# A first router whose bias goes through the matrix unit, whose gates ScalarE scales, and whose rows are stored and loaded in two batches

## The chip, the cores and the metric

One core of a Trainium2 chip runs the program. The metric is the device time of one execution in microseconds (us); lower is better. The engines are named as the profile names them: PE is the matrix unit (PEld its weight loads), DVE is VectorE, ACT is ScalarE, POOL is GpSimd, and SP issues the transfers.

## What is computed

Two transformer layers on x of 2 x 1024 tokens of width 128, all in float32 with a residual sum after each of four parts. Of the parts the change touches the second, a mixture of 160 experts of which each token takes 8:

```
logits = x @ router_w.T + expert_bias
probs  = sigmoid(logits)
top_w, top_idx = top_k(probs, 8)
top_w  = top_w / (sum(top_w) + 1e-9) * 2.5
combine[token, top_idx] = top_w
h1  = silu(einsum('th,eih->eti', x, w_gate)) * combine.T[:, :, None]
out = einsum('eti,ehi->th', h1, w_down) + silu(x @ w_gate_shared.T) @ w_down_shared.T
```

Here x is the layer norm of the residual. The first part is attention with 16 heads of width 8, the third a memory that is updated in 16 steps, the fourth a mixture of 8 experts with a router of its own.

## The kernel before

The four parts run one after the other. The 2048 tokens are 16 tiles of 128 rows, worked on in G = 4 groups of 4 tiles (512 tokens). The order of the work is written out by hand per engine: each engine has its own program, the programs meet at counting semaphores, and within an engine everything runs in the order written.

**Norm.** `norm(1)` makes the layer norm before the first mixture. DVE computes statistics and `xn` group by group (L1440 to L1452), PE transposes each group into bank 0 or 1 (L1027), and ACT copies the bank twice, to `xh` (rounded to the fast matmul type, L810) and to `xnT` (L811). DVE then makes the low parts `xl = xnT - xh` of all four groups (`low_x`, L1467). In the expert loop every product is three products: xh by both weight parts, xl by the high one.

**First router.** PE makes the logits of a group, four products of 160 columns (`router_logits`, L1224), in two banks of a pair of `wide`; group g + 2 reuses the banks of group g. DVE adds the bias into `gates` (L1654), ACT takes the sigmoid in place (L931). Only after all four bias sums does DVE choose: per group four MAX8 (L1660), four MATCH_REPLACE that strike out the eight largest (L1667), sum, epsilon, reciprocal and factor (L1668 to L1671), then `left = max(left, 0) - gates` (L1673), which leaves minus the chosen gates, and a multiply by the factor of the token (L1675). Meanwhile PE and ACT do the shared expert in banks 4 and 5 (L1234, silu L939, L1214). When a group is chosen PE transposes its 4 x 160 columns (L1247, L1248), and ACT copies them out as `cT_first` (128 experts) and `cT_last` (32 experts, L943, L944).

**Rows through DRAM.** SP stores each group's columns to `c_dram` (L586, L588). Once all eight stores have landed it loads rows back, spread over the partitions: one load of 1 MB per pair of experts (`load_rows`, L571) into one of CB = 4 buffers `cb`.

**Expert loop.** 80 pairs of experts by 4 groups are 320 steps. In a step PE makes three products into one of four banks (L1259), ACT the silu (L958), DVE multiplies by the row (L1693), ACT rounds to `hh` (L952), DVE makes `hl` (L1685), and PE accumulates a low product (L1266) and two high ones (L1272) of earlier steps. PE's low product in iteration n waits until DVE has ended step n - 2. PE begins the loop when `cT_ready` is complete and all `xl` are there.

The second router (layer 2) uses the same `norm` and `low_x` in `norm(3)`.

## Time and profile before

| what | value |
|---|---|
| median of 3 runs | 1117.31 us (1117.04 to 1119.65) |
| profiled execution, its own time | 1117.76 us |
| its span (first to last instruction) | 1115.8 us |
| PE, DVE, ACT, POOL busy | 93%, 75%, 72%, 20% of the span |
| attention ends, first router's stage, expert loop starts | about 340, 350 to 391, 391 |
| second router's stage | about 934 to 968 |
| PE's share of the chain that ended last | 82% |

Busy shares are averages over stages. In the two expert loops and in attention PE is nearly always busy. The stage that the change rewrites is some 40 us long, and there the chain of waits runs over DVE and the transfers. [...]

### The profile page before, as it was taken

Reading aid. Unit: us, or ns where it says so; the run is one execution under the profiler, and the core shown is the slowest. Engines: PE = TensorE matmul, PEld = TensorE weight load, DVE = VectorE, ACT = ScalarE, POOL = GpSimd, SP = SyncE. Lnnn points to the kernel's source line nnn. Section 1 sums busy time; section 2 is a strip of 40 time slices with the busy share of each in tenths; the row PEclk is TensorE's granted clock in tenths of the full one; section 3 lists DMA queues with packets and bytes.
Section 4 is the critical chain, followed back from the end, with each engine's and each line's share of the span. In section 5 each row is a group of like instructions: output and inputs, shape, how many; then the busy total and the mean of one; then the engine's idle time right before and its main releaser. Section 6 shows DMA issues by size and latency. Waiting matters only on the chain.

```text
span 1115.8 us, 20193 instructions
## 1 busy us (share of the span) xinstructions
PE 1039.4 (93%) x5244; PEld 688.9 (62%) x5244; DVE 831.3 (75%) x1965; ACT 804.8 (72%) x1310; POOL 222.3 (20%) x326
## 2 busy tenths in 40 slices
PE   5899999999996589999999999999998998799997
PEld 3222222232325278888888888888876777587785
DVE  8544444343345779999999999999986887598897
ACT  6599999999992468787878787877774443266664
POOL 3767664444442000000000000000004112000000
PEclk9799999999997899999999999999999998799999
DMA  4368776666661176666666666666621000123321
GB/s 142 116 213 259 221 235 204 208 208 216 210 211 42 36 301 238 235 244 244 240 249 239 239 237 235 240 248 245 239 79 41 1 1 1 59 99 117 111 86 38
DMA packets 91894, 190.43 MB, mean 171 GB/s; under 512 B 10700, under 2 KB 55372, under 8 KB 81612
## 3 DMA queue, kind: packets, MB, share of 16 engines
q1 hardware_dynamic: 91860, 190.05, 49.9%
q8 instruction: 12, 0.20, 0.1%
q14 instruction: 22, 0.18, 0.1%
HBM read 154.03 MB, written 35.98 MB: 170 GB/s over the span
## 4 chain that ended last, share of the span: by engine, by line
PE 82%; DVE 8%; ACT 4%; issue 3%; DMA 2%; POOL 2%; ACTq 0%; DVEq 0%; SPq 0%; POOLq 0%
PE bank L1259 26%; PE bank L1272 15%; PE bank L1129 10%; PE bank L1266 8%; PE bank L1111 6%; PE bank L1114 6%; ACT ring L897 2%; PE bank L1361 2%; PE bank L1140 1%; POOL m_norm L786 1%; PE bank L1345 1%; DVE xn L1452 1%; DMA ring<-c_rows 1%; DVE stats L1440 1%; PE bank L1077 1%
## 5 line engine op out<-in xcount | busy, mean ns | idle before, releaser
L897 ACT ACTIVATE ring<-bank,minus_bound 128x1024 f32<-128x1024 f32 x256 | 271.4, 1111 | 22.9 <-DVE bank L1553 11.9
L1259 PE MATMUL bank<-xh,w_parts 128*128 128x512 f32 x896 | 277.2, 391 | 1.9 <-DVEq L1679 1.9
L958 ACT ACTIVATE bank<-bank 128x512 f32<-128x512 f32 x320 | 186.2, 582 | 90.8 <-PE bank L1259 90.8
L1693 DVE TENSOR_TENSOR bank<-bank,ring 128x512 f32<-128x512 f32 x320 | 223.9, 700 | 29.7 <-DMA ring<-c_rows 6.8
L1272 PE MATMUL bank<-hh,w_parts 128*128 128x512 f32 x776 | 239.7, 390 | 0.0
L1685 DVE TENSOR_TENSOR hl<-bank,hh 128x512 fp32r<-128x512 f32 x321 | 218.6, 681 | 0.1
L1553 DVE TENSOR_TENSOR bank<-bank,corner 128x128 f32<-128x128 f32 x256 | 76.6, 299 | 170.4 <-PE bank L1114 170.2
L952 ACT ACTIVATE hh<-bank 128x512 fp32r<-128x512 f32 x321 | 190.4, 593 | 3.2 <-DVE bank L1693 3.1
L1259 PEld LDWEIGHTS bank<-xh,w_parts 128*128 128x128 f32 x896 | 167.9, 188 | 38.0 <-DVEq L1679 2.3
L1259 PE MATMUL bank<-xl,w_parts 128*128 128x512 f32 x448 | 174.7, 390 | 0.0
L1272 PEld LDWEIGHTS bank<-hh,w_parts 128*128 128x128 f32 x776 | 145.9, 188 | 30.6 <-ACT hh L952 0.4
L1266 PE MATMUL bank<-hl,w_parts 128*128 128x512 f32 x390 | 153.5, 394 | 6.5 <-DVE hl L1685 6.4
L1129 PE MATMUL bank<-ring,v_cur 128*32 128x512 f32 x1024 | 137.2, 608 | 0.7 <-ACT ring L897 0.7
L1114 PE MATMUL bank<-q_stack,k_stack 128*128 128x512 bf16 (+3 forms) x384 | 106.7, 333 | 1.5 <-ACTq L890 1.5
L1111 PE MATMUL bank<-q_stack,k_stack 128*128 128x384 bf16 (+2 forms) x320 | 98.3, 323 | 7.4 <-ACT ring L897 3.4
L1259 PEld LDWEIGHTS bank<-xl,w_parts 128*128 128x128 f32 x448 | 84.4, 188 | 17.7
L766 POOL MEMSET ring<- 128x512 f32 x1 | 0.5, 531 | 473.1 <-PE bank L1266 473.1
L1111 PEld LDWEIGHTS bank<-q_stack,k_stack 128*128 128x128 bf16 x320 | 30.7, 97 | 97.6 <-ACT ring L897 92.1
L1266 PEld LDWEIGHTS bank<-hl,w_parts 128*128 128x128 f32 x390 | 73.4, 188 | 26.9 <-DVE hl L1685 12.0
L1114 PEld LDWEIGHTS bank<-q_stack,k_stack 128*128 128x128 bf16 x384 | 34.0, 99 | 58.2 <-ACT ring L897 28.5
L1008 ACT ACTIVATE q_stack<-bank 128x512 f32<-128x512 f32 x64 | 38.2, 597 | 27.3 <-PE bank L1259 25.5
L952 ACT ACTIVATE hh<-q_stack 128x512 fp32r<-128x512 f32 x65 | 41.0, 630 | 16.6 <-DVE q_stack L1849 15.5
(281 smaller groups left out, 1135.4 us busy)
## 6 DMA issues: line engine op xcount, KB each, us to landing
ring<-c_rows SPq DMA_DIRECT2D x80, 1024.0 KB, 5.0
w_parts<-w_pairs SPq DMA_DIRECT2D x160, 128.0 KB, 2.5
w_pairs<-xh SPq DMA_DIRECT2D x16, 768.0 KB, 4.4
q_stack<-q_parts SPq DMA_DIRECT2D x64, 144.0 KB
k_stack<-k_parts SPq DMA_DIRECT2D x192, 48.0 KB
w_pairs<-xl SPq DMA_DIRECT2D x16, 512.0 KB, 2.9
ring<-c_rows SPq DMA_DIRECT2D x16, 512.0 KB, 4.6
big<-in_w_exp SPq DMA_DIRECT2D x16, 384.0 KB, 4.8
```

The lines of the kernel that those rows point to most:

```text
L897: act.activation(ring[:, c % RING * S:(c % RING + 1) * S], wide[c % 2][:], ACT.Exp, bias=minus_bound[:]).then_inc(exp_done, 1)
L952: act.activation(hh[(c - 1) % 2][:], hidden, ACT.Copy).then_inc(split, 1)
L958: act.activation(bank(4 + c % ZB), bank(4 + c % ZB), ACT.Silu).then_inc(silu_ready, 1)
L1111: ins = pe.matmul(wide[c % 2][:, lo:mid], k_stack[0][u][:, keys], q_stack[1][u][:, lo:mid], start=True, stop=True)
L1114: ins = pe.matmul(wide[c % 2][:, mid:hi], k_stack[1][u][:, keys], q_stack[0][u][:, mid:hi], start=True, stop=True)
L1129: ins = pe.matmul(bank(4 + u)[at:at + 32, :], v_cur[u][:, done_step % QT, :], ring[:, at_ring + h * 512:at_ring + (h + 1) * 512], start=(d ...
L1259: ins = pe.matmul(out_, w[i], x_[j], start=start and k == 0, stop=stop and k == 2, skip_group_check=not start)
L1266: return pe.matmul(bank(done_step % G), w[0], hl[done_step % 2][:], start=False, stop=False, skip_group_check=True)
L1272: ins = pe.matmul(bank(done_step % G), part, hh[done_step % 2][:], start=False, stop=False, skip_group_check=True)
L1553: dve.tensor_tensor(tile, tile, corner[:], ALU.mult).then_inc(corner_done, 1)
L1685: dve.tensor_tensor(hl[(c - 1) % 2][:], hidden, hh[(c - 1) % 2][:].bitcast(F32), ALU.subtract).then_inc(split, 1)
L1693: dve.tensor_tensor(bank(4 + c % ZB), bank(4 + c % ZB), cb[u][:, g * GW:(g + 1) * GW], ALU.mult).then_inc(hid_ready, 1)
```

## The change

- **Bias.** PE opens each group's logit banks with two products of a row of ones by the bias (320 columns each, `router_biases`), and the logits accumulate on top. Those of groups 0 and 1 stand ahead of `norm(1)`; those of groups 2 and 3 wait for the sigmoid of groups 0 and 1. ACT takes the sigmoid directly from the banks (`take_logits`), between its copies of xnT. The DVE sums are gone. The sigmoid table is loaded early by a one-column activation.
- **High and low parts of x.** ACT makes `xh` from `xnT` after the last sigmoid (`high_x`); DVE makes the low parts after the choice. The same holds for the second router, where `high_x` follows one group behind.
- **Choice.** Epsilon and factor are one instruction and the multiply by the factor is gone from DVE: ACT scales each tile (`Copy` with a scale per token, 16 instructions of 160 columns). `rest` has four buffers instead of two.
- **Shared expert.** All four silus come before the scaling, in banks 2 and 3, and the four down products follow in one piece, ahead of the transposes.
- **Copies.** ACT alternates scaling and copying; `cT_last` of the last group is copied by DVE.
- **Rows.** SP stores groups 0 and 1, waits for them to land, loads their half of the rows for all four buffers (4 x 512 KB), stores groups 2 and 3, waits, and loads the other half. DVE waits for a half at the first and third step of each pair. In the loop each row load is two of 512 KB.
- Several semaphores of the unused slow attention path share those of the fast path.

SP's transfers between the router and the loop, before:

```order
L586 DMA c_rows<-xn 128x512 [waits cT_ready]
L588 DMA c_rows<-fold 32x512 [waits cT_ready]
L586 DMA c_rows<-xn 128x512 [waits cT_ready]
L588 DMA c_rows<-fold 32x512 [waits cT_ready]
L586 DMA c_rows<-xn 128x512 [waits cT_ready]
L588 DMA c_rows<-fold 32x512 [waits cT_ready]
L586 DMA c_rows<-xn 128x512 [waits cT_ready]
L588 DMA c_rows<-fold 32x512 [waits cT_ready]
L571 DMA ring<-c_rows 128x1x2048 [waits c_saved]
L571 DMA ring<-c_rows 128x1x2048 x3
```

and with the change:

```order
L593 DMA c_rows<-xn 128x512 [waits cT_ready]
L594 DMA c_rows<-fold 32x512
L593 DMA c_rows<-xn 128x512 [waits cT_ready]
L594 DMA c_rows<-fold 32x512
L575 DMA ring<-c_rows 128x1x1024 [waits c_saved]
L575 DMA ring<-c_rows 128x1x1024 x3
L593 DMA c_rows<-xn 128x512 [waits cT_ready]
L594 DMA c_rows<-fold 32x512
L593 DMA c_rows<-xn 128x512 [waits cT_end,cT_ready]
L594 DMA c_rows<-fold 32x512
L575 DMA ring<-c_rows 128x1x1024 [waits c_saved]
L575 DMA ring<-c_rows 128x1x1024 x3
```

Four row loads and a wait for `c_saved` now stand ahead of the stores of groups 2 and 3.

ACT from the end of attention to the loop, with the change (xn in L957 is `cT_first`, fold in L959 is `cT_last`):

```order
L823 ACTIVATE xh<-xnT 128x512 [waits xnT_ready] x3
L951 ACT_TABLE_LOAD [waits shared_psum]
L951 ACTIVATE q_stack<-bank 64x512 [waits moe_zero]
L951 ACTIVATE q_stack<-bank 64x512 [waits shared_psum]
L951 ACTIVATE k_stack<-bank 64x512 [waits shared_psum] x2
L964 ACTIVATE ring<-ring,top_inv 128x160 [waits combine_ready]
L964 ACTIVATE ring<-ring,top_inv 128x160 x3
L964 ACTIVATE ring<-ring,top_inv 128x160 [waits combine_ready]
L964 ACTIVATE ring<-ring,top_inv 128x160 x3
L957 ACTIVATE xn<-bank 128x512 [waits cT_psum]
L959 ACTIVATE fold<-bank 32x512
L964 ACTIVATE ring<-ring,top_inv 128x160 [waits combine_ready]
```

The copies of a group stand behind the silus and behind the scaling of the next group; before, only the silus stood ahead of them.

The diff, cut to its core:

```diff
@@ -172,9 +172,10 @@
-        rest = [ring[:, (5 + u) * S:(5 + u) * S + TPG * NE].rearrange("p (t e) -> p t e", t=TPG) for u in range(2)]
+        rest = [ring[:, (2 * g + 1) * S:(2 * g + 1) * S + TPG * NE].rearrange("p (t e) -> p t e", t=TPG) for g in range(G)]
         top = sb("top", [P, NT, 8])
         top_sum = sb("top_sum", [P, NT])
+        early_table = sb("early_table", [P, 1])
         top_inv = sb("top_inv", [P, NT])
@@ -204,6 +205,7 @@
         act_out = [q_stack[0][u][:].bitcast(F32) for u in range(2)]
+        shared_hid = act_out + [k_stack[0][u][:].bitcast(F32) for u in range(2)]
         hid = [q_stack[1][u][:].bitcast(F32) for u in range(2)]
...
...
@@ -566,9 +570,10 @@
-            def load_rows(m, u):
-                sp.dma_start(cb[u], bass.AP(c_dram.tensor, m * (2 * T), [[0, EI], [T, 2], [1, T]])).then_inc(cb_loaded[u], 16)
+            def load_rows(m, u, h):
+                sp.dma_start(cb[u][:, h * S:(h + 1) * S], bass.AP(c_dram.tensor, m * (2 * T) + h * S, [[0, EI], [T, 2], [1, S]]))\
+                    .then_inc((cb_early, cb_loaded)[h][u], 16)
@@ -582,18 +587,21 @@
                 cols = slice(g * GW, (g + 1) * GW)
-                sp.wait_ge(cT_ready, 2 * g + 1)
+                sp.wait_ge(cT_ready, min(2 * g + 2, 2 * G - 1))
+                if g == G - 1:
+                    sp.wait_ge(cT_end, 1)
                 sp.dma_start(c_dram[0:P, cols], cT_first[:, cols]).then_inc(c_saved, 16)
-                sp.wait_ge(cT_ready, 2 * g + 2)
                 sp.dma_start(c_dram[P:NE, cols], cT_last[:, cols]).then_inc(c_saved, 16)
-            sp.wait_ge(c_saved, 2 * G * 16)
-            for u in range(CB):
-                load_rows(u, u)
+                if g % 2:
+                    sp.wait_ge(c_saved, 2 * (g + 1) * 16)
+                    for u in range(CB):
+                        load_rows(u, u, g // 2)
                     sp.wait_ge(hid_ready, i * (CB * G) + ((u + 1) * G + CREDIT))
-                    load_rows(i * CB + (CB + u), u)
+                    for h in range(2):
+                        load_rows(i * CB + (CB + u), u, h)
                     sp.wait_ge(low_used, i * (CB * G) + ((u + 1) * G + 3 + CREDIT))
@@ -799,20 +807,20 @@
-            def norm(k):
+            def norm(k, follow):
                 for g in range(G):
                     cols = slice(g * GW, (g + 1) * GW)
-                    if k == 1 and g == 0:
-                        act.wait_ge(w_saved[0], 16 + NH // 2 * 16)
-                    if k % 2:
-                        act.activation(xh[:, cols], bank(n % 2), ACT.Copy)
                     act.activation(xnT[:, cols], bank(n % 2), ACT.Copy).then_inc(xnT_ready, 1)
-                    if k == 2 and g:
-                        token_gates(g - 1)
-                if k == 2:
-                    token_gates(G - 1)
+                    if g:
+                        follow(g - 1)
+            def high_x(g, k=3):
+                cols = slice(g * GW, (g + 1) * GW)
+                act.wait_ge(xnT_ready, G * k + g + 1)
+                act.activation(xh[:, cols], xnT[:, cols], ACT.Copy).then_inc(xh_ready, 1)
@@ -924,24 +932,40 @@
-            norm(1)
-            for g in range(G):
-                ts = slice(g * TPG, (g + 1) * TPG)
-                act.wait_ge(logit_ready, g + 1)
-                act.activation(gates[:, ts, :], gates[:, ts, :], ACT.Sigmoid).then_inc(gate_ready, 1)
+            act.activation(early_table[:], half[:, 0:1], ACT.Sigmoid)
+            def take_logits(g):
+                act.wait_ge(logit_psum, g + 1)
+                act.activation(gates[:, g * TPG:(g + 1) * TPG, :].rearrange("p (b t) e -> p b t e", b=2),
+                               logits1(g).rearrange("p b (t e) -> p b t e", t=2), ACT.Sigmoid).then_inc(gate_ready, 1)
+            norm(1, take_logits)
+            take_logits(G - 1)
+            act.wait_ge(w_saved[0], 16 + NH // 2 * 16)
+            for g in range(G):
+                high_x(g, 1)
+            act.wait_ge(moe_zero, 1)
             for g in range(G):
                 act.wait_ge(shared_psum, g + 1)
-                if g >= 2:
-                    act.wait_ge(shared_down, g - 1)
-                if g < 2:
-                    act.wait_ge(moe_zero, 1)
-                act.activation(act_out[g % 2][0:EI], bank(4 + g % 2)[0:EI, :], ACT.Silu).then_inc(shared_act, 1)
-            for g in range(G):
+                act.activation(shared_hid[g][0:EI], bank(2 + g % 2)[0:EI, :], ACT.Silu).then_inc(shared_act, 1)
+            def take_cT(g):
                 act.activation(cT_first[:, cols], bank(4 + g % 2), ACT.Copy).then_inc(cT_ready, 1)
-                act.activation(cT_last[:, cols], bank(6 + g % 2)[0:NE - P, :], ACT.Copy).then_inc(cT_ready, 1)
+                if g < G - 1:
+                    act.activation(cT_last[:, cols], bank(6 + g % 2)[0:NE - P, :], ACT.Copy).then_inc(cT_ready, 1)
+            for g in range(G):
+                act.wait_ge(combine_ready, g + 1)
+                for t in range(TPG):
+                    act.activation(rest[g][:, t, :], rest[g][:, t, :], ACT.Copy, scale=top_inv[:, g * TPG + t:g * TPG + t + 1])\
+                        .then_inc(scaled_ready, 1)
+                if g:
+                    take_cT(g - 1)
+            take_cT(G - 1)
             act.sem_inc(silu_ready, CREDIT)
...
@@ -993,9 +1018,10 @@
-            norm(3)
+            norm(3, high_x)
             act.wait_ge(shifted, 1)
             act.activation(soft[:], soft[:], ACT.Exp).then_inc(exp2_ready, 1)
+            high_x(G - 1)
             act.wait_ge(c2T_psum, 1)
@@ -1209,46 +1235,51 @@
-            def shared_sum(g):
-                pe.wait_ge(shared_act, g + 1)
-                pe.matmul(bank(g), wd_shared[:], act_out[g % 2][0:EI], start=True, stop=False, skip_group_check=True)\
-                    .then_inc(shared_down, 1)
+            def router_biases(g):
+                row_ = b_router[0:1, :]
+                for b in range(2):
+                    pe.matmul(logits1(g)[:, b, :], ones[0:1, :], bass.AP(row_.tensor, row_.offset, [list(row_.ap[0]), [0, 2], [1, NE]]),
+                              start=True, stop=False, skip_group_check=True)
                 pe.wait_ge(xnT_ready, G + g + 1)
-                if g >= 2:
-                    pe.wait_ge(logit_ready, g - 1)
                 for t in range(TPG):
                     ins = pe.matmul(logits1(g)[:, t // 2, t % 2 * NE:(t % 2 + 1) * NE], xnT[:, (g * TPG + t) * P:(g * TPG + t + 1) * P],
-                                    w_router[:], start=True, stop=True)
+                                    w_router[:], start=False, stop=True, skip_group_check=True)
                 ins.then_inc(logit_psum, 1)
+                if g < G - 2:
+                    pe.wait_ge(gate_ready, g + 1)
+                    router_biases(g + 2)
+            for g in range(2):
+                router_biases(g)
             norm(1, router_logits)
             for g in range(G):
+                if g == 0:
+                    pe.wait_ge(x_ready, G)
                 if g >= 2:
                     pe.wait_ge(shared_act, g - 1)
+                pe.matmul(bank(2 + g % 2)[0:EI, :], w_shared[:], xnT[:, g * GW:(g + 1) * GW], start=True, stop=True)\
+                    .then_inc(shared_psum, 1)
+            pe.wait_ge(shared_act, G)
+            for g in range(G):
+                pe.matmul(bank(g), wd_shared[:], shared_hid[g][0:EI], start=True, stop=False, skip_group_check=True)
+            for g in range(G):
                 if g == 0:
-                    pe.wait_ge(logit_ready, G)
-                pe.matmul(bank(4 + g % 2)[0:EI, :], w_shared[:], xnT[:, g * GW:(g + 1) * GW], start=True, stop=True)\
-                    .then_inc(shared_psum, 1)
-                if g:
-                    shared_sum(g - 1)
-            shared_sum(G - 1)
-            for g in range(G):
-                pe.wait_ge(combine_ready, g + 1)
-                if g == 0:
-                    pe.wait_ge(shared_act, G)
-                    pe.wait_ge(logit_ready, G)
+                    pe.wait_ge(gate_ready, G)
                 if g >= 2:
                 for t in range(TPG):
-                    pe.transpose(bank(4 + g % 2)[:, t * P:(t + 1) * P], rest[g % 2][:, t, 0:P], ident[:])
-                    ins = pe.transpose(bank(6 + g % 2)[0:NE - P, t * P:(t + 1) * P], rest[g % 2][:, t, P:NE], ident[:])
+                    pe.wait_ge(scaled_ready, g * TPG + t + 1)
+                    pe.transpose(bank(4 + g % 2)[:, t * P:(t + 1) * P], rest[g][:, t, 0:P], ident[:])
+                    ins = pe.transpose(bank(6 + g % 2)[0:NE - P, t * P:(t + 1) * P], rest[g][:, t, P:NE], ident[:])
                 ins.then_inc(cT_psum, 1)
             pe.wait_ge(moe_zero, 1)
-            pe.wait_ge(cT_ready, 2 * G)
+            pe.wait_ge(cT_ready, 2 * G - 1)
+            pe.wait_ge(cT_end, 1)
             pe.wait_ge(xl_ready, G)
@@ -1454,14 +1485,10 @@
                         ins.then_inc(xn_ready, 1)
-                if k % 2:
-                    for g in range(G):
-                        low_x(k, g)
                 cols = slice(g * GW, (g + 1) * GW)
-                dve.wait_ge(xnT_ready, G * k + g + 1)
+                dve.wait_ge(xh_ready, k // 2 * G + g + 1)
                 if k == 1 and g == 0:
@@ -1645,13 +1672,6 @@
             norm(1)
-            dve.wait_ge(w1_loaded, 4 * 16)
-            bias4 = bass.AP(b_router[:].tensor, b_router[:].offset, [list(b_router[:].ap[0]), [0, 2], [0, 2], [1, NE]])
-            for g in range(G):
-                dve.wait_ge(logit_psum, g + 1)
-                v = gates[:, g * TPG:(g + 1) * TPG, :].rearrange("p (b t) e -> p b t e", b=2)
-                dve.tensor_tensor(v, logits1(g).rearrange("p b (t e) -> p b t e", t=2), bias4, ALU.add).then_inc(logit_ready, 1)
             for g in range(G):
@@ -1659,22 +1679,21 @@
                 link.wait()
-                if g >= 2:
-                    dve.wait_ge(cT_psum, g - 1)
-                left = rest[g % 2]
+                left = rest[g]
                 for t in tiles:
                 link(dve.tensor_reduce(top_sum[:, ts], top[:, ts, :], AX.X, ALU.add))
-                link(dve.tensor_scalar(top_sum[:, ts], top_sum[:, ts], 1e-9, None, ALU.add))
-                link(dve.reciprocal(top_inv[:, ts], top_sum[:, ts]))
-                link(dve.tensor_scalar(top_inv[:, ts], top_inv[:, ts], -ROUTED, None, ALU.mult))
-                link(dve.scalar_tensor_tensor(left[:, :, :], left[:, :, :], 0.0, gates[:, ts, :], ALU.max, ALU.subtract))
-                inv = top_inv[:, ts]
-                dve.tensor_tensor(left[:, :, :], left[:, :, :],
-                                  bass.AP(inv.tensor, inv.offset, [list(inv.ap[0]), list(inv.ap[1]), [0, NE]]), ALU.mult).then_inc(combine_ready, 1)
-            dve.wait_ge(cT_ready, 2 * G)
+                link(dve.tensor_scalar(top_sum[:, ts], top_sum[:, ts], 1e-9, -1.0 / ROUTED, ALU.add, ALU.mult))
+                link.sign(dve.reciprocal(top_inv[:, ts], top_sum[:, ts]))
+                link.wait()
+                dve.scalar_tensor_tensor(left[:, :, :], left[:, :, :], 0.0, gates[:, ts, :], ALU.max, ALU.subtract).then_inc(combine_ready, 1)
+            for g in range(G):
+                low_x(1, g)
+            dve.wait_ge(cT_psum, G)
+            dve.tensor_copy(cT_last[:, (G - 1) * GW:G * GW], bank(6 + (G - 1) % 2)[0:NE - P, :]).then_inc(cT_end, 1)
+            dve.wait_ge(cT_end, 1)
+            dve.wait_ge(cT_ready, 2 * G - 1)
             dve.memset(bank(4 + ZB - 1), 0.0).then_inc(hid_ready, CREDIT)
@@ -1687,8 +1706,8 @@
                     n, u, g = i * (CB * G) + c, c // G, c % G
-                    if g == 0:
-                        dve.wait_ge(cb_loaded[u], i * 16 + 16)
+                    if g % 2 == 0:
+                        dve.wait_ge((cb_early, cb_loaded)[g // 2][u], i * 16 + 16)
                     ready(dve, silu_ready, n)
@@ -1829,6 +1848,8 @@
             dve.tensor_tensor(combine2[:], combine2[:], by_row(r_sum[:], NE2), ALU.mult).then_inc(combine2_ready, 1)
+            for g in range(G):
+                low_x(3, g)
             dve.wait_ge(c2T_psum, 1)
```

## Rows read from the trace of the kernel before

**Rows 1.** Chain that ended last, stretch 365 to 440: start us, us, what.
```profile
390.19 2.17 DMA c_rows<-fold
...
392.37 5.23 DMA ring<-c_rows
```
**Rows 2.** Timeline, DVE, 360 to 374: start, us, engine line op.
```profile
361.12 1.89 DVE L1467 TENSOR_TENSOR xl<-xnT,xh 128x512 fp32r<-128x512 f32 x3
...
364.18 1.55 DVE L1654 TENSOR_TENSOR big<-bank,b_router 128x640 f32<-128x640 f32 x2
...
368.34 0.99 DVE L1660 MAX8 top<-big 128x8 f32<-128x160 f32 x4
...
372.24 0.83 DVE L1675 TENSOR_TENSOR ring<-ring,top_inv 128x640 f32<-128x640 f32 x1
```
**Rows 3.** Timeline, PE and ACT, 357 to 378 (x8: four products).
```profile
357.88 2.34 PE L1224 MATMUL bank<-w_router,xnT 128*128 128x160 f32 x8
...
360.73 1.25 PE L1224 MATMUL bank<-w_router,xnT 128*128 128x160 f32 x8
...
361.82 0.60 PE L1027 MATMUL bank<-ident,xn 128*128 128x128 f32 x4
...
365.03 1.47 ACT L931 ACTIVATE big<-big 128x640 f32<-128x640 f32 x2 [0.19 <-DVE big L1654]
...
369.21 1.28 ACT L939 ACT_TABLE_LOAD   x1
...
372.20 1.07 PE L1234 MATMUL bank<-xnT,w_shared 128*64 128x512 f32 x2
...
373.31 0.59 ACT L939 ACTIVATE q_stack<-bank 64x512 f32<-64x512 f32 x1 [1.73 <-PE bank L1234]
...
375.25 1.98 PE L1214 MATMUL bank<-q_stack,wd_shared 64*128 64x512 f32 x4
```
**Rows 4.** Timeline, ACT: two copies of a bank, and two scaled copies at 867.
```profile
389.10 0.60 ACT L943 ACTIVATE xn<-bank 128x512 f32<-128x512 f32 x1 [4.47 <-PE bank L1248]
389.59 0.57 ACT L944 ACTIVATE fold<-bank 32x512 f32<-32x512 f32 x1
...
867.25 0.90 ACT L993 ACTIVATE ring<-state,steps 128x256 f32<-128x256 f32 x2
```
**Rows 5.** Timeline, SP, 388 to 396: the four row loads before the loop.
```profile
392.37 2.49 SPq L571 DMA_DIRECT2D ring<-c_rows  x4
```
**Rows 6.** DMA issues at 392.4, at 393.7 to 394.5, and at 970.2: KB each, median us to landing.
```profile
ring<-c_rows SPq DMA_DIRECT2D x1, 1024.0 KB, 5.2
...
ring<-c_rows SPq DMA_DIRECT2D x2, 1024.0 KB, 10.6
...
ring<-c_rows SPq DMA_DIRECT2D x1, 512.0 KB, 4.2
```
**Rows 7.** Timeline: PE's third low product, third multiply of the expert loop, PE's fifth low product.
```profile
399.06 0.50 PE L1266 MATMUL bank<-hl,w_parts 128*128 128x512 f32 x1 [2.70 <-DVE hl L1685]
...
400.12 0.69 DVE L1693 TENSOR_TENSOR bank<-bank,ring 128x512 f32<-128x512 f32 x1
...
401.92 0.39 PE L1266 MATMUL bank<-hl,w_parts 128*128 128x512 f32 x1
```
**Rows 8.** Stretches: us, PE, PEld, DVE, ACT, POOL busy, PE's clock, DMA share, GB/s.
```profile
350.00:352.50 2.50, 0.03 (x1) 0.00 (x0) 2.40 (x12) 0.00 (x0) 0.37 (x2) 1.00 0.00 0
352.50:355.00 2.50, 0.21 (x1) 0.24 (x2) 2.15 (x13) 0.00 (x0) 2.19 (x3) 0.75 0.00 0
...
393.00:395.00 2.00, 2.00 (x7) 1.58 (x6) 0.00 (x0) 0.70 (x2) 0.00 (x0) 0.57 0.67 172
...
397.00:399.00 2.00, 0.00 (x0) 0.00 (x0) 1.28 (x3) 0.55 (x2) 0.00 (x0) 1.00 1.06 446
```
**Rows 9.** Part 5 of the page, the row multiply of the expert loop.
```profile
L1693 DVE TENSOR_TENSOR bank<-bank,ring 128x512 f32<-128x512 f32 x320 | 223.9, 700 | 29.7 <-DMA ring<-c_rows 6.8
```
**Rows 10.** Timeline, DVE, around the second router.
```profile
950.40 0.29 DVE L1801 TENSOR_REDUCE r_max<-bank 128x16 f32<-128x128 f32 x1 [1.40 <-PE bank L1378]
...
966.50 1.21 DVE L1833 COPY fold<-bank 8x1024 f32<-8x1024 f32 x1 [3.67 <-PE bank L1386]
```

23 lines of the change are left out of this document (13 added, 10 removed).

## The prediction

> **What bounds the kernel now.** I read the page first: PE is busy 93% of the span and has 82% of the chain, so only a stage in which PE waits can be shortened. The chain of the stretch 365 to 440 shows one: from the end of the norm to the expert loop the chain runs over DVE's choice and then over two transfers, the last store of the rows (2.17 us) and the first load (5.23 us) [rows 1]. The timeline shows what DVE does there. It is free of the norm at 361.1, makes four low parts at 0.63 apiece, then four bias sums of some 0.8, and begins to choose only at 368.3; a group takes from 368.34 to 373.07, 4.7 us [rows 2], and the fourth ends at 387.05. The columns are out at 390.2, the rows are there at 397.6 [rows 1], DVE makes its third multiply of the loop at 400.12 and PE its fifth low product at 401.92 [rows 7]. From then on PE goes at its own pace, some 1.4 a step (two from 399.06 to 401.92 [rows 7]), so what PE's fifth low product gains or loses is what the program gains or loses. I follow the change to that instruction.
>
> **Gates.** ACT now has only one copy of a group ahead of the sigmoid, but PE and ACT take turns: bias products of group g + 2 wait for the sigmoid of group g, and the transposes of the next groups are queued behind them. PE's first four products are unchanged and end at 360.2 (357.88 + 2.34, at the low clock) [rows 3]. Two bias products have 640 columns in float32, as four logit products have, so 1.25 [rows 3]. The sum from 360.2: sigmoid 0.74, bias 1.25, transposes 0.60, logits 1.25, sigmoid 0.74, bias 1.25, transposes 0.60, logits of groups 2 and 3 2.50, sigmoid 0.74 [rows 3], and some 0.2 of handovers: the last gates are ready at 370.1, those of group 2 at 368.9.
>
> **Choice.** DVE begins at 361.2 instead of 368.3, since low parts and bias sums no longer stand ahead. A group loses one small operation and the multiply of 0.83 [rows 2], 4.7 - 1.05 = 3.65. Groups 0 and 1 end at 368.5, group 2 waits 0.4 for its gates, the fourth ends at 376.2: 10.9 us earlier than before. The four low parts follow until 378.8. If that were the path, the change would be worth some 10 us. It is not the path, because of what stands on ACT.
>
> **ACT and PE behind the gates.** From 370.1 ACT makes four high parts, 0.49 from start to start [rows 4], until 372.2, and loads the silu table, 1.28 [rows 3], until 373.5. The shared expert has two banks: silu 0.59, PE's third product 1.07, its fourth 1.0, silu 0.59 [rows 3], with handovers 3.4, until 376.9. The four down products were interleaved and hidden before; now they stand in one piece ahead of the transposes: 4 x 0.99 (1.98 for two [rows 3]) until 380.9. Transposes of group 0: 1.0, until 381.9. ACT has meanwhile scaled groups 0 and 1. Its two copies of group 0 take 1.06 [rows 4], until 383.0. Then it scales group 2: the price of a scaled copy of 160 columns is not in the trace; two of 256 columns take 0.90, 0.40 from start to start [rows 4], which is the upper bound, and 0.25, the same per column, the lower. I take 0.31, since part of it is fixed, so 1.3, until 384.3 (bounds 1.0 and 1.6). Copies of group 1 until 385.4, scaling of group 3 until 386.7, copies of group 2 until 387.7, of group 3 until 388.3 (its second copy is DVE's). PE can begin the loop at about 388.4, 2.5 us earlier than before, and not 10.
>
> **Rows.** Stores of groups 0 and 1 are issued by 385.9 and landed 2.17 later [rows 1], at 388.0. SP issues four loads, 2.3 to 2.5 us [rows 5], until 390.4, and only then the four stores of groups 2 and 3, the last at 391.8. They stand behind 2.1 MB of loads. Issued one after the other, the first of the old loads landed after 5.2, the last two after 10.6 in the middle [rows 6]: transfers of this queue wait for those ahead. At the 446 GB/s of [rows 8] 2.1 MB flow 4.7 us, and a load of 1 MB that lands after 5.2 has 2.4 of flow and 2.8 of fixed time, so the loads are through at 388.0 + 2.8 + 4.7 = 395.5, and the stores (655 KB) about 1.5 later, at 397.0. Without any queueing they would have landed at 391.8 + 2.2 = 394.0; the lower bound is that, the upper 398. The nearest row is that of the loads, so I take 397.0. The second halves land 4.2 later [rows 6], and DVE's third multiply comes at 401.3 instead of 400.12. PE's fifth low product needs a multiply and a low part more, 1.35 (0.69 and 0.66 of DVE [rows 7, 2]), so 402.65 instead of 401.92: +0.7. What the halves bring is that two steps are done before; what they cost is that the second batch is queued behind the first.
>
> [...]
>
> **PE's clock at the restart.** PE can do five iterations' first products before it needs the third multiply. It begins at 388.4 and is through at about 396, then stands idle some 6 us. In the trace an idle time of 2.7 us ahead of 399.06 [rows 7] left the clock at 1.00 in 397 to 399, but after a stop at 350.0 it was 0.75 on average in 352.5 to 355, and the loop, begun at 390.9 with the clock down, still had 0.57 in 393 to 395 [rows 8]. [...]
>
> **What costs nothing.** Bias products of groups 0 and 1 (2.5 us at full clock) lie between 350.0 and 354.8, where PE is idle [rows 8]. The early table load lies in ACT's wait for the norm. The four low parts after the choice (2.5) end before DVE's copy and its wait for ACT; without that cover they would cost 2.5. The 80 additional waits of DVE in the loop lie in its idle time, 29.7 us over 320 multiplies [rows 9], and are for halves that came long before; the 80 additional row loads cost SP 0.55 each, and SP waits for PE and DVE all through the loop. In the second router low parts leave the time ahead of the maximum, but DVE waits there for PE's logits until 950.40 anyway, 1.40 idle, and they enter a wait of 3.67 before 966.50 with 2.5 [rows 10]: nothing either way. If PE's transposes there ended 1.2 earlier, they would show.
>
> **Sum.** +0.7 and +1.9 are +2.6 on the profiled execution's own 1117.76, or 1120.4; that execution lies 0.45 above the median of the runs, so I forecast 1119.9, against 1117.31. About 0.3%, 3.4 us, is what a measurement of this kernel can tell from no change, so the forecast is "no difference that can be told", on the slow side. Its own range, from the bounds of the store, the scaling and the clock, is 1115.5 to 1120.6.
>
> **Rivals.**
> *Choice is the path (faster).* If the silus and down products are done before the second group is chosen, the copies follow the choice. For it: DVE is on the chain for 20 us now and does 11 us less ahead of the last group. Against: ACT's list in the order printed, where silus, scaling and copies have one fixed order from 370.1 on. In full it would give 376.2 + 1.3 + 1.0 + 1.1, columns out at 379.6 instead of 390.2, 10.6 less: 1106.7. A milder form is likelier: stores that don't queue (-3.0 on my sum), no loss at the restart (-1.9) and the first logits at the full clock because the bias products ran just before (2.34 becomes 1.25, -1.1): 1119.9 - 6.0 = 1113.9. Together 0.20.
> *PE goes cold before the shared expert (slower).* Between its second shared product, which ends at 371.4, and the first silu at 374.1 PE has nothing to do. That is 2.7 us, after little work. If the clock falls, products three and four take 2.1 each instead of 1.07, ACT's last silu and all behind it come about 1.8 later: 1121.7. It decides as soon as 0.8 us is added to my sum, and bias products at the low clock (2.3 instead of 1.25, once) would do it too, with 1.1. For it: the whole stage gives PE short pieces between waits. Against: the idle time ahead of 399.06, as long, left it at 1.00 [rows 7, 8]. 0.34.
> *The halves bring nothing and cost nothing*, or the stage ends where it did because ACT is late: columns out at 390, and rows 1 us later or earlier. That is inside the forecast's range and part of its 0.46.
>
> **Numbers.** No change to be told: 0.46; faster 0.20; slower 0.34. The range 1113.5 to 1123.5 takes in the mild faster case and the slower one with 1.8 more, and leaves out the full gain of 10 us and a double loss. I say 1119.9.
>
> **What would show it.** DVE's first MAX8 at 361.2 and its fourth group done at about 376; ACT's last silu at 376.9 (378.7 in the slower rival); first copy of columns at 381.9; last at 388.3; SP's first row load at 388.0 and its fifth at 397; third multiply at 401.3; PE's clock at 0.50 for some 4 us after it. Wrong if the first copy comes before 379 (then the choice is the path), if the fifth row load is issued before 395 (then the stores do not queue behind the loads), or if a step of the loop is longer than before, because then the waits or halves do cost in the loop, where 0.01 a step is 3.2 us.

## The result and the profile after

| | median us | ratio to before, 95% interval |
|---|---|---|
| before | 1117.31 (1114.27 to 1119.65, 5 runs) | |
| changed kernel | 1127.38 (1123.28 to 1128.49, 5 runs) | 1.0083 [1.0055, 1.0111] |

The change makes the kernel some 9 to 10 us slower; the prediction had 1119.9, in a range of 1113.5 to 1123.5. The profiled execution of the changed kernel took 1128.34 with a span of 1126.6, 10.8 over the span of before. DVE's norm ends at 360.2 in it, 0.9 earlier than before [rows 2], so from there on 11.7 are to be found.

The page's part 5 has the row multiply, the answer to [rows 9]: 8.8 us more of idle time, and 7.1 more of waits for transfers.

```profile
L1712 DVE TENSOR_TENSOR bank<-bank,ring 128x512 f32<-128x512 f32 x320 | 223.9, 700 | 38.5 <-DMA ring<-c_rows 13.9
```

Stretches of the changed kernel, PE alone: stretch, length, PE busy, granted clock, DMA share, GB/s.

```profile
355.00:357.50 2.50, 1.46 (x7) 0.50 0.00 0
360.00:362.50 2.50, 2.42 (x4) 0.50 0.00 0
370.00:372.50 2.50, 2.50 (x11) 0.50 0.00 0
375.00:377.50 2.50, 1.00 (x3) 1.00 0.01 3
```

The granted clock is 0.50 from 355 to 372.5, that is through the whole of the gates. In the kernel before it was 0.50 from 357.5 to 360, but 1.00 while the second group's logits were made (360.73 to 361.98), which took 1.25 [rows 3]. The timelines of PE and ACT show what that does (the four logit products of a group stand there as x8, a pair of bias products as x4, four transposes as x4):

```profile
360.08 2.50 PE L1244 MATMUL bank<-b_router,ones 1*128 1x320 f32 x4 [0.79 <-ACT big L940]
362.51 1.11 PE L1053 MATMUL bank<-ident,xn 128*128 128x128 f32 x4
369.88 4.26 PE L1250 MATMUL bank<-w_router,xnT 128*128 128x160 f32 x16
```
```profile
374.18 0.70 ACT L940 ACTIVATE big<-bank 128x640 f32<-128x640 f32 x1 [1.22 <-PE bank L1250]
374.78 2.18 ACT L823 ACTIVATE xh<-xnT 128x512 fp32r<-128x512 f32 x4
376.98 1.28 ACT L951 ACT_TABLE_LOAD   x1
381.38 2.65 ACT L964 ACTIVATE ring<-ring,top_inv 128x160 f32<-128x160 f32 x8
386.28 0.60 ACT L957 ACTIVATE xn<-bank 128x512 f32<-128x512 f32 x1 [2.26 <-PE bank L1278]
391.72 0.57 ACT L957 ACTIVATE xn<-bank 128x512 f32<-128x512 f32 x1
```

Bias products take 2.50 a pair, transposes 1.11 a group, and the logits of group 1 take 2.34. The last sigmoid ends at 374.9 instead of the 370.1 forecast. Behind it ACT's list goes as forecast, one piece after the other, and the columns are out at 392.3.

How cold the gates are differs from one execution to the next, though. Three of the runs below leave the gates as the changed kernel has them. In the first the last sigmoid ends 12.7 behind DVE's norm, and in the fifth and in the one with one early load the last sigmoids are these:

```profile
370.91 0.70 ACT L941 ACTIVATE big<-bank 128x640 f32<-128x640 f32 x1 [0.38 <-PE bank L1257]
372.94 0.70 ACT L944 ACTIVATE big<-bank 128x640 f32<-128x640 f32 x1 [1.43 <-PE bank L1254]
```

They end 11.4 and 10.0 behind the norm. In the execution shown here it is 14.7, the coldest of the four: over 355 to 372.5 its granted clock was 0.50 on average, and 0.62, 0.68 and 0.73 in the first run, the fifth and the one with one early load. The forecast had 9.0.

Then SP and the chain of waits (DMA rows: from issue to landing), the answer to [rows 1, 5]:

```profile
392.22 2.50 SPq L575 DMA_DIRECT2D ring<-c_rows  x4
394.76 0.83 SPq L593 DMA_DIRECT2D c_rows<-xn  x1
395.63 0.91 SPq L594 DMA_DIRECT2D c_rows<-fold  x1
396.63 1.04 SPq L593 DMA_DIRECT2D c_rows<-xn  x1
```
```profile
389.99 2.21 DMA c_rows<-fold
397.71 7.70 DMA c_rows<-fold
405.43 3.88 DMA ring<-c_rows
```

The stores of group 1 land after 2.21, as before. The last one, issued at 397.71 behind four loads, lands after 7.70, at 405.4; the fourth of these loads, issued at 394.10, landed after 9.7, at 403.8. The first of the second halves comes at 409.3, and until then the loop stands (DVE, then PE, the answer to [rows 7]):

```profile
397.34 0.69 DVE L1712 TENSOR_TENSOR bank<-bank,ring 128x512 f32<-128x512 f32 x1
409.42 0.70 DVE L1712 TENSOR_TENSOR bank<-bank,ring 128x512 f32<-128x512 f32 x1 [10.79 <-DMA ring<-c_rows]
410.76 0.79 PE L1297 MATMUL bank<-hl,w_parts 128*128 128x512 f32 x1 [9.70 <-DVE hl L1704]
```

PE's fifth low product comes at 410.76 instead of 401.92 [rows 7], 8.8 later. That product takes 0.79 instead of 0.39: PE restarts at a granted clock of 0.50 (409 to 413; it is 0.56 in 413 to 415 and 1.00 in 415 to 417). Another 2.1 are lost until it is back at 1.36 a step, for PE's last low product of the loop starts at 844.5 instead of 833.6, 10.9 later. Behind the loop nothing is added.

**How runs are compared below.** DVE's norm ends anywhere from 359.3 to 364.3 in the profiled executions, whatever was changed behind it. So beside the ratio of the medians I use the length of the stretch that the change touches, from the end of that norm to the start of PE's last low product of the loop: 472.4 before (361.1 to 833.6), 484.3 in the changed kernel. A single profiled execution can lie up to 4.7 us from the median of its kernel (the fifth run and the last variant), so the ratio decides; all ratios are to the kernel before. The difference of two ratios is uncertain by some 0.003, an estimate from their intervals, or 3 to 4 us.

### The profile page after: what moved, and what is told of

It reads as the page before. It is cut to its first block, busy times and chain, and to the rows that moved or that the text cites. A ratio compares the mean times of both kernels' runs of the same rounds, so it can differ in the third digit from the quotient of the medians.

```text
span 1126.6 us, 20455 instructions
## 1 busy us (share of the span) xinstructions
PE 1048.4 (93%) x5260; PEld 694.7 (62%) x5260; DVE 825.5 (73%) x1954; ACT 810.0 (72%) x1326; POOL 222.4 (20%) x326
## 4 chain that ended last, share of the span: by engine, by line
PE 82%; DVE 6%; ACT 5%; issue 2%; DMA 2%; POOL 2%; SPq 1%; ACTq 0%; DVEq 0%; POOLq 0%
PE bank L1290 26%; PE bank L1303 15%; PE bank L1155 10%; PE bank L1297 8%; PE bank L1137 6%; PE bank L1140 6%; ACT ring L905 2%; PE bank L1392 2%; PE bank L1166 1%; DMA c_rows<-fold 1%; POOL m_norm L794 1%; PE bank L1376 1%; DVE xn L1483 1%; PE bank L1053 1%; PE bank L1250 1%
## 5 line engine op out<-in xcount | busy, mean ns | idle before, releaser
L905 ACT ACTIVATE ring<-bank,minus_bound 128x1024 f32<-128x1024 f32 x256 | 271.3, 1111 | 21.5 <-DVE bank L1580 12.7
```

The costliest lines, as they stand in the source:

```text
L905: act.activation(ring[:, c % RING * S:(c % RING + 1) * S], wide[c % 2][:], ACT.Exp, bias=minus_bound[:]).then_inc(exp_done, 1)
```

## The experiments

**The loads behind all stores.**

```diff
-                if g % 2:
-                    sp.wait_ge(c_saved, 2 * (g + 1) * 16)
-                    for u in range(CB):
-                        load_rows(u, u, g // 2)
+            sp.wait_ge(c_saved, 2 * G * 16)
+            for u in range(CB):
+                for h in range(2):
+                    load_rows(u, u, h)
```

> The changed kernel with all eight stores first and the row loads, still in halves, behind them. Theory A (the first batch of loads, put between the stores, costs the 8.8 us that PE's fifth low product is late after the columns are 2.1 late): columns out at 392.3 as in the changed kernel, last store landed 394.9, loads issued from there, first multiply at 400 and third at 402, PE's fifth low product at 404 instead of 410.8, span 6 to 8 us under the changed kernel's 1126.6, so 1118.5 to 1120.5 and about 1120 us in time. Rival B (waits and halves in the loop cost, or stores alone are slow): span 1124 or more.

Measured: 1120.23, ratio 1.0047 [1.0028, 1.0066], stretch 474.9. Its chain has the store and the first load next to each other again, and the store lands in 2.41:

```profile
390.24 2.41 DMA c_rows<-fold
392.67 3.90 DMA ring<-c_rows
```

The stretch gets 9.4 of its 11.9 us back. But this profiled execution is the fastest of its eight (1117.92), and 2.0 of the 9.4 are not the loads': the clock was up for a moment in this run's gates (0.92 in 357.5 to 360; last sigmoid 12.7 behind the norm, not 14.7). That leaves at most 7.4 for the early loads; by the medians they are 0.0036 of 0.0083, or 4 us, less than half. Either way it is less than the 8.8 of the theory. The rest of the loss is looked for in the late columns.

**Fillers that keep PE busy in the gates.** They write a bank that nothing reads.

```diff
+            def fill(columns):
+                pe.matmul(bank(3)[:, 0:columns], ident[:], fold[:, 0, 0:columns], start=True, stop=True)
...
+            pe.wait_ge(x_ready, G)
+            for _ in range(2):
+                fill(GW)
-            norm(1, router_logits)
+            norm(1, router_logits, lambda g: fill(GW) if g == 0 else None)
...
                 if g < G - 2:
+                    fill(2 * NE)
                     pe.wait_ge(gate_ready, g + 1)
```

> The changed kernel plus filler products of no use on TensorE (bank 3, ident by fold) behind the first bias products, between the transposes and ahead of each wait for a sigmoid. Theory A (the granted clock of 0.50 in 355 to 372.5 makes the gates 4.8 us late): clock 0.9 or more in that stretch, bias products 1.25 a pair, transposes 0.60, last sigmoid at 369 to 371 instead of 374.9, columns out about 4.5 earlier, third multiply as much earlier, time 1122 to 1123.5 us. Rival B (the gates are late for the turns between PE and ACT, not for the clock): fillers raise the clock or not, but the last sigmoid stays at 373 or later and the time at 1126 or more.

Measured: 1123.51, ratio 1.0067 [1.0045, 1.0089], stretch 482.3. By the medians that is a gain of 0.0016, inside the noise. Two stretches (PE alone, columns as above), the fillers' kernel first, then the changed one:

```profile
355.00:372.50 17.50, 14.08 (x66) 0.99 0.00 0
372.50:385.00 12.50, 11.82 (x28) 0.50 0.01 2
```
```profile
355.00:372.50 17.50, 14.87 (x46) 0.50 0.00 0
372.50:385.00 12.50, 8.91 (x23) 0.95 0.00 1
```

The first step of the theory holds, and by more than expected: the last sigmoid starts at 365.99 instead of 374.18, and ends 7.1 behind the norm. The rest doesn't follow, because in this execution the clock falls behind the gates, where PE waits 2.91 for the first silu, and the down products run at 0.50. The same wait of 2.91 left the clock at 1.00 in the changed kernel; why it fell here is open. In its chain the down products take

```profile
373.85 7.19 PE bank L1279 x8
394.26 0.51 SPq L594 DMA_DIRECT2D c_rows<-fold  x1
```

7.19 where the changed kernel has 3.70. This is the slower rival of the prediction, at work in a neighbour of the changed kernel. The last store, issued at 394.26 behind the four loads as before, landed 8.1 later: the slow landing repeats. (The profiled execution, 1126.03, is one of the slower two of its six.)

**Both edits.**

The two diffs above, together.

> Both edits, all stores first and fillers on TensorE. Theory A (two separate costs that add): last sigmoid about 370, columns out about 388, first multiply 395.5, span about 12 under the changed kernel's, time 1114 to 1116 us, so 1 to 3 under the kernel before. Rival B (they share a cause): no more than the better of the two alone, 1118 or more.

Measured: 1116.00, ratio 1.0003 [0.9989, 1.0017], stretch 469.6. The clock held at 1.00 from 372.5 to 385 here, and the last store was issued at 387.3. So the early loads and the missing work on PE together account for the whole loss. By the medians the first edit alone gives 0.0036, the second alone 0.0016, both 0.0080. That this is more than the sum would fit the second run, where the low clock moved to the down products, but the 0.0028 over the sum is inside the noise of four ratios, and here the same PE program as the second run's kept the clock up. The ratio to the kernel before is 1.0003; the expected 1 to 3 us under it are not to be seen.

**The kernel before with the two batches alone.** In it group 1 is chosen 10 us ahead of group 3.

```diff
+                if g % 2:
+                    sp.wait_ge(c_saved, 2 * (g + 1) * 16)
+                    for u in range(CB):
+                        load_rows(u, u, g // 2)
-            sp.wait_ge(c_saved, 2 * G * 16)
-            for u in range(CB):
-                load_rows(u, u)
```

The row loads in the loop are halves too, and each group has a buffer of its own for the rest, as in the changed kernel.

> The kernel before with the row loads in two batches alone (halves, first halves behind the stores of group 1, second behind those of group 3; each group its own buffer for the rest). Here group 1 is done some 10 us ahead of group 3, so the first batch is through before the last stores. Theory A (a batch costs only where its loads are still moving when the last stores are issued): stores of group 3 land at 392.4 as before, second halves 4.2 later, third multiply 397 to 398 instead of 400.1, time 1114 to 1115.5 us. Rival B (splitting the loads costs by itself, with more packets or more waits): time 1118 or more.

Measured: 1116.03, ratio 1.0001 [0.999, 1.0013], stretch 470.2. The third multiply is at 396.9, as expected, but the median is over the expected range, and the gain is not to be seen in it. Early loads and stores meet even here, with the stores of group 2 and then with those of group 3. SP's queue and, below, two stretches (PE alone) show it:

```profile
381.10 2.50 SPq L572 DMA_DIRECT2D ring<-c_rows  x4
383.64 0.65 SPq L588 DMA_DIRECT2D c_rows<-xn  x1
388.13 0.34 SPq L588 DMA_DIRECT2D c_rows<-xn  x1
392.80 7.50 SPq L572 DMA_DIRECT2D ring<-c_rows  x6
```
```profile
382.00:392.00 10.00, 4.67 (x14) 0.52 0.92 274
385.00:388.00 3.00, 1.97 (x8) 0.50 0.97 221
```

The fourth load of the batch, issued at 383.0, landed 7.9 later, at 390.9; by the sum of the prediction (2.8 + 4.7 from the first issue) it would be 388.6. The last store, issued before that at 388.59, lands after 4.19 instead of 2.17. Theory A as I wrote it ("a batch costs only where its loads are still moving when the last stores are issued") stands, but its "through before the last stores" was wrong.

**Stores on another queue.** ACT issues the four stores of groups 2 and 3 itself, so that no load stands ahead of them in their queue.

```diff
             take_cT(G - 1)
+            act.wait_ge(cT_ready, 2 * G - 1)
+            act.wait_ge(cT_end, 1)
+            for g in range(2, G):
+                cols = slice(g * GW, (g + 1) * GW)
+                act.dma_start(c_dram[0:P, cols], cT_first[:, cols]).then_inc(c_late, 16)
+                act.dma_start(c_dram[P:NE, cols], cT_last[:, cols]).then_inc(c_late, 16)
```

> The changed kernel; the first loads stay where they are, but the four stores of groups 2 and 3 are issued by ScalarE on its own queue, so that no load stands ahead of them in their queue. Theory A (they land 7.70 us after issue because they stand behind the loads in SP's queue): landed 2.2 to 3.5 after the last issue, second batch of loads issued at about 398 instead of 405.4, third multiply at 402 instead of 409.4, time 1119 to 1121 us. Rival B (the 16 DMA engines or the memory are shared, so that loads under way slow the stores in any queue): landing 6 or more, time 1125 or more.

Measured: 1122.32, ratio 1.0041 [1.0024, 1.0057], between the two forecasts. The profiled execution is the slowest of its eight, with the down products at 7.19 again, so its stretch of 482.9 says little. Its landing says more:

```profile
396.28 7.07 DMA c_rows<-fold
403.37 3.90 DMA ring<-c_rows
```

7.07 after issue, on a queue with nothing but stores ahead, where theory A had 2.2 to 3.5. So theory A falls, and with it the reason that the prediction gave: the stores are not late because loads stand ahead of them in their queue, they share something with them. The landing of the last store even comes before that of the fourth load (issued at 396.2, landed 8.2 later).

But the other queue does give something: the issue. It takes 1.8 us from the first to the last of the four stores, and none of them stands behind SP's 2.5 of loads. From the issue of the first load to the landing of the last store it is 9.0 here (394.32 to 403.4) and 13.2 in the changed kernel (392.22 to 405.4). Of these 4.2 us, 3.5 are the earlier issue and 0.6 the shorter landing. By the medians the run gains 0.0042 on the changed kernel, as much as the first run.

**Half loads alone.** The kernel before, with each load in two halves, all behind the stores.

```diff
             for u in range(CB):
-                load_rows(u, u)
+                for h in range(2):
+                    load_rows(u, u, h)
```

> The kernel before with each row load split in two halves of 512 KB, all of them behind all stores, nothing else. Theory A (halves cost DMA time, 0.73 instead of 0.66 busy in the loop, that PE never sees): first multiply 0.7 to 1.0 earlier (first landing 4.4 instead of 5.2), loop at the same 1.36 a step, time 0.5 to 1 us under the kernel before, within what can be told. Rival B (that part of what the batched loads won is lost in the loop): 2 us or more over the kernel before.

Measured: 1116.44, ratio 0.9988 [0.9973, 1.0004], stretch 471.2. The first multiply comes at 395.1, 6.3 behind the issue of the last store at 388.8; in the kernel before it is 7.5 (397.7 and 390.2). Halves cost nothing that PE sees. They do cost DMA time. This is the loop in this kernel, then in the one before:

```profile
420.00:820.00 400.00, 400.00 (x1765) 1.00 0.73 238
```
```profile
420.00:820.00 400.00, 400.00 (x1765) 1.00 0.66 239
```

The run also has a row that the prediction lacked, loads in halves ahead of the loop with no store among them:

```profile
394.00:402.00 8.00, 6.52 (x29) 1.00 1.02 375
```

Here the fourth half load, issued at 392.8, landed after 7.3, which is 9.1 behind the issue of the first at 390.96.

**One early load instead of four.**

```diff
-                if g % 2:
+                if g == 1:
                     sp.wait_ge(c_saved, 2 * (g + 1) * 16)
-                    for u in range(CB):
-                        load_rows(u, u, g // 2)
+                    load_rows(0, 0, 0)
```

The other seven halves follow once all eight stores have landed.

> The changed kernel with only one half load (0.5 MB) between the stores of group 1 and of group 2 instead of four, the other seven behind all stores. Theory A (stores share the DMA engines with what is under way, so they are late by the bytes ahead of them): last store landed 3 to 4.5 after its issue, between 2.2 with none and 7.7 with four, time 1121 to 1123 us. Rival B (any read of the rows under way costs the stores the full 5 us): landing 6 or more, time 1125 or more.

Measured: 1120.84, ratio 1.0050 [1.0031, 1.0068], just under the expected range, stretch 472.9. Its chain:

```profile
393.16 4.34 DMA c_rows<-fold
397.52 4.20 DMA ring<-c_rows
```

2.2 to 2.4 with no load ahead, 4.34 with 0.5 MB, 7.70 with 2 MB: the landing grows with what is under way. Theory A holds in its landing. The ratio gains 0.0033 on the changed kernel, which can't be told from the first run's 0.0036.

**The shared expert behind the columns.** This is built on the third run's kernel; it is called the eighth kernel, after its label. All stores come first, and there are fillers, some more of them between the transposes. PE makes the shared products into banks 0 to 3, the fourth behind the last transposes. The table, the four silus and the down products come after the last copy, and DVE scales groups 2 and 3.

```diff
-            for g in range(G):
-                act.wait_ge(shared_psum, g + 1)
-                act.activation(shared_hid[g][0:EI], bank(2 + g % 2)[0:EI, :], ACT.Silu).then_inc(shared_act, 1)
...
+            for g in range(G):
+                take_cT(g)
+            for g in range(G):
+                act.wait_ge(shared_psum, g + 1)
+                act.activation(shared_hid[g][0:EI], bank(g)[0:EI, :], ACT.Silu).then_inc(shared_act, 1)
```

> All stores first and fillers as in the third run, and the shared expert out of ScalarE's way: products of the four groups into banks 0 to 3, their silus, the silu table and the down products behind the copies of the columns, the scaling of groups 2 and 3 back on VectorE. Theory A (the columns are held up by ScalarE's list, high parts, table, four silus, 16 scalings, seven copies, and not by the choice): columns out at 380.5 to 382 instead of 386.9, first multiply at 388.5 to 390 instead of 394.1, PE busy with the shared expert while the rows are fetched and warm at the start of the loop, time 4 to 8 us under the third run's, 1108 to 1112 us. Rival B (PE's transposes or the choice hold the columns, or the silus behind them come too late for the first expert): no more than 2 us under it, 1114 or more.

Measured: 1104.21, ratio 0.9885 [0.9863, 0.9907], stretch 461.7. It beats both kernels and lies 4 us under the expected range. ACT's timeline:

```profile
366.81 2.18 ACT L823 ACTIVATE xh<-xnT 128x512 fp32r<-128x512 f32 x4
377.17 0.60 ACT L953 ACTIVATE xn<-bank 128x512 f32<-128x512 f32 x1 [2.44 <-PE bank L1289]
377.79 1.28 ACT L967 ACT_TABLE_LOAD   x1
```

The last copy is at 377.2 instead of 391.7, now behind DVE's choice. Not all of these 14 us are the new order's. Counted from DVE's norm to the last of ACT's copies of columns, it is 32.1 in the changed kernel, 30.0 in the first run, 24.5 in the third, which has the same gates and stores as this one, and 18.0 here. So the new order, with the fillers that came with it, gives 6.5 of them. Over the third run it gives 7.9 by the stretch and 0.0118 by the medians, or 12 to 13 us; beside the earlier columns it has PE's clock at 1.00 from 377 to 395, over the whole start of the loop, where the third run's fell to 0.50 (396 to 398) behind a wait of 4.64. The chain goes on through the table and

```profile
379.73 3.70 PE bank L1295 x8
383.43 0.91 PE bank L1306 x3
```

the down products straight into the loop, at a clock of 1.00. The first rows land at 384.7, and the first multiply, at 385.0, was released by ACT's silu and not by the rows. So the choice can be the path of the columns, as the faster rival had it, once the shared expert is out of ACT's list.

**Two variants of it.** In the eighth kernel ACT scales groups 0 and 1; here first all four groups, then three.

```diff
-            for g in range(2):
+            for g in range(G):
                 act.wait_ge(combine_ready, g + 1)
```

> The eighth kernel with the scaling of all four groups on ScalarE, as the changed kernel has it. Theory A (what held the columns up was the shared expert and its table in ScalarE's list, not the scaling): the fourth group is scaled by 1.3 on ScalarE instead of 0.83 on VectorE and VectorE chooses 0.83 sooner, columns out within 1 us of the eighth kernel's, time 1103.5 to 1105.5 us. Rival B (the scaling is a main part of the delay): columns out 2 us or more later, time 1106 or more.

Measured: 1105.02, ratio 0.9906 [0.9886, 0.9926], stretch 462.0, last store issued 18.5 after the norm, as in the eighth kernel.

```diff
-            for g in range(2):
+            for g in range(3):
                 act.wait_ge(combine_ready, g + 1)
```

> The eighth kernel with the scaling of group 2 on ScalarE too, so that VectorE scales group 3 alone. Theory A (there the chain is VectorE's choice, then the copy, the stores and the loads): the fourth choice and the columns come 0.8 earlier, time 0.5 to 1 us under the eighth kernel's, 1103 to 1104 us, which can hardly be told from it. Rival B (ScalarE becomes the bound again): columns later, 1105 or more.

Measured: 1105.51, ratio 0.9909 [0.9892, 0.9925], stretch 460.7, last store 17.7 after the norm. The store is 0.9 earlier, as theory A has it; the median lies in rival B's range, but neither variant can be told from the eighth kernel. The scaling was not what held the columns up.

**The eighth kernel without fillers.**

```diff
-            for _ in range(2):
-                fill(GW)
-            norm(1, router_logits, lambda g: fill(GW) if g == 0 else None)
+            norm(1, router_logits)
...
-            fill_x(GW)
             pe.wait_ge(gate_ready, G)
```

The fillers between the transposes and ahead of the waits for a sigmoid go too.

> The eighth kernel (shared expert behind the columns) without any filler product. Theory A (short pieces between waits let PE's clock fall, the order alone doesn't keep it up): granted clock 0.5 to 0.7 in 355 to 370, last sigmoid 4 to 5 us later than with fillers (366.2), the fourth choice and the columns 2 to 4 later, the loop's start may be cold too, time 1107 to 1111 us. Rival B (with the order of the eighth kernel PE has enough work of its own): clock over 0.9 there and time within 1.5 us of the eighth kernel's 1104.

Measured: 1109.56, ratio 0.9941 [0.9919, 0.9964]. The clock falls in the gates, 0.73 on average (0.98 with fillers):

```profile
355.00:372.50 17.50, 12.73 (x57) 0.73 0.00 1
```

By the medians the fillers are worth 5 to 6 us (0.0056, clear of the noise). The profiled execution doesn't show where: its stretch is 462.2, only 0.5 over that with fillers, and its last store is issued 19.2 behind the norm instead of 18.5, where 2 to 4 us were expected. It had a late norm (363.4), and its clock was back up (0.92 in 362.5 to 365, 1.00 in 365 to 367.5) before it fell again (0.50 in 370 to 372.5). So the fillers' worth is shown by the medians, and its place is open.

## Why the prediction was wrong

In the profiled executions the forecast had PE's fifth low product at 402.65, and it came at 410.76, 8.1 later. Two steps failed, each for about half of that: the columns were 4.0 late, and the rows took 4.2 more from there.

**Failed: "Gates", the sum from 360.2.** It took only PE's first four products at a clock of 0.50 and everything after at 1.00, since the kernel before had 1.00 from 360.73 to 377.5. The terms were right in form and about half as large as they should have been: bias 2.50 for 1.25, transposes 1.11 for 0.60, logits 2.34 for 1.25 and 4.26 for 2.50. The gates came at 374.9, 4.8 late, with an earlier start. I had named this ("bias products at the low clock"), but priced it at one bias product, 1.1, while here the whole alternation of PE and ACT, from 355 to 372.5, ran at 0.50. The second run shows that the clock is the cause of the late gates: with more work on PE the clock is 0.99 and the last sigmoid is 7.1 behind the norm instead of 14.7. The size is partly chance: the same gates ended 10.0 to 14.7 behind the norm in four executions, all over the 9.0 forecast, and the one profiled here was the worst. What the late columns cost the program is shown by the third run against the first (0.0044 by the medians), not by the second alone.

**Failed: "Rows", stores landed at 397.0, upper bound 398.** From the first early load to the last store's landing the forecast had 9.0 (388.0 to 397.0); it took 13.2 (392.2 to 405.4). The term that was too small is the loads' flow. I had them through 7.5 behind the first issue, at 446 GB/s, a rate of 1 MB loads alone [rows 8]; the fourth landed after 11.6. Of these 4.1, some 1.6 come in the sixth run too, where halves flow with no store among them (9.1), and some 2.5 come with the stores. The stores then landed 1.6 behind the loads, for 1.5 forecast. SP also took longer to issue the stores, 0.83, 0.91, 1.04 and 0.51 instead of some 0.4 each. Side by side loads and stores moved as in the first of these stretches, of the changed kernel; the second is of the kernel before, where only 1 MB loads flow:

```profile
394.00:404.00 10.00, 7.06 (x24) 0.83 0.88 261
```
```profile
395.00:404.00 9.00, 6.30 (x28) 1.00 1.01 421
```

Loads in halves alone had 375 (sixth run). The reason I gave, order within the queue, is not borne out by the fifth run: with stores alone in their queue the landing is 7.07. But 261 is no fixed rate of mixed traffic either, for there nearly the same bytes moved at

```profile
396.00:403.00 7.00, 5.98 (x21) 0.76 1.00 360
```

What differs is the stores' queue and how soon they are issued. What makes the loads slower when SP issues the stores behind them is open. The trace before has no row of mixed traffic, so the bound should have been wider.

**Wrong: the sum's own range.** With its bounds (store at 394.0 or 398, scaling 0.3 either way, 0 or 3.8 for the clock, an estimate of mine) it is about 1114.7 to 1123.1 and not 1115.5 to 1120.6. The measured 1127.4 lies outside both.

**Right in size: the restart.** The sum has +1.9 for it, an estimate of mine that no run shows as such. The changed kernel showed a clock of 0.50 in 409 to 413 and 0.56 in 413 to 415, and 2.1 lost until PE was back at 1.36 a step.

**Right: ACT's list is the path, not the choice.** From the last sigmoid to the first copy of columns the forecast had 11.8 (370.1 to 381.9); it took 11.4 (374.9 to 386.3). The eighth kernel shows the same from the other side: with silus and downs out of the list the columns are 6.5 us earlier than in the third run.

**Right: what costs nothing.** Extra waits, halves and the second router: the loop keeps 1.36 a step, and the span behind it is the same. The sixth run confirms the halves.

**The rivals.** The slower one, PE cold before the shared expert, did not happen in the profiled execution of the changed kernel (clock 1.00 at 375 to 377.5), but did in those of the second (0.50 in 372.5 to 385) and the fifth run (0.50 in 377.5 to 385), at 3.5 us a time for the down products alone (7.19 for 3.70). The fifth has the changed kernel's own PE program, so this is a matter of the execution, and the changed kernel can pay it too. It was priced at 1.8 for two shared products; the down products, which follow, pay more. The mild faster one lost on all three of its terms.

## What to carry to other kernels

When a change makes a matrix unit wait for another engine between short pieces, price the whole stage at both of the clocks that the traces show, not the first piece only: a pair of bias products took 2.50 at 0.50 here and 1.34 at 1.00. Before putting early loads between stores that something waits for, ask what the two do to each other side by side: another queue brought the stores' issue forward by 3.5 us here, but the last still landed 7.07 after it. And when a stage has one engine with a fixed list, look for the part of the list that nobody needs until later; here the shared expert, moved into the wait for the rows, was worth 12 to 13 us by the medians. And one profiled execution is not the kernel: here the same program had its gates ready anywhere from 10.0 to 14.7 us behind the norm.

## What the runs showed of the hardware

- Stores and half loads under way together, all issued by SP, moved at 261 GB/s with the DMA engines 0.88 busy; with the stores issued by ACT nearly the same bytes moved at 360 with 1.00 busy (fifth run). Half loads alone had 375 with 1.02 (sixth run), 1 MB loads alone 421 with 1.01 (the kernel before). The landing of a 64 KB store rose from 2.2 to 4.3 and 7.7 us with 0, 0.5 and 2 MB of loads issued ahead, and was 7.1 from a queue of its own. Whether engines or memory set this was not tried.
- In the changed kernel SP's issue of a store took 0.34 to 0.43 us ahead of the loads. Right behind four loads it took 0.83, 0.91 and 1.04, and 0.51 for the fourth store.
- PE's clock stayed at 0.50 through 17.5 us (355 to 372.5) in which PE was busy for 14.87 in the changed kernel, and was 0.99 in the second run's with 14.08 busy. The two busy times are not the same amount of work, since a pair of bias products took 2.50 at 0.50 and 1.34 at 1.00.
- The same program of PE did not get the same clock in each execution: in the down products behind a wait of 2.91 us it was 1.00 in the changed kernel and 0.50 in the fifth run, and 1.00 in the third run and 0.50 in the second.
- The same bytes in loads of 512 KB instead of 1 MB kept the DMA engines 0.73 busy instead of 0.66 (238 and 239 GB/s, sixth run and kernel before, 420 to 820).
